# A graph network on one core: second edge bias in PSUM by ScalarE, edge layers in quarters, window additions first

## The reference, cut to what matters

```
h   = leaky(x @ W1[l] + b1[l]) @ W2[l] + b2[l]            # per node
e   = leaky(edge_attr @ We1[l] + be1[l]) @ We2[l] + be2[l] # per edge
msg = h[src] * e * dot_scale[l]
agg = segment_sum(msg, dst)
x   = layernorm(x + agg * res_w[l]) * ln_g[l] + ln_b[l]
```

## Time and profile before

| | |
|---|---|
| median of three runs | 6618.61 us |
| profiled execution, its own time | 6615.82 us |
| its span | 6614.0 us |
| busy: TensorE, VectorE, GpSimd, ScalarE | 85%, 78%, 68%, 17% |
| chain that ended last, by engine | TensorE 54%, VectorE 21%, issue 15%, ScalarE 3% |
| granted TensorE clock, mean | 0.88 of 2.4 GHz |

### The profile page before, as it was taken

How to read it: one execution, slowest core, us unless ns; L and a number is a source line. 1 busy time by engine, 2 the same in 40 slices (tenths; PEclk the granted TensorE clock), 3 DMA queues, 4 the chain that set the end, 5 groups by cost and what they waited for, 6 DMA issues and landing times.

```text
span 6614.0 us, 169076 instructions
## 1 busy us (share of the span) xinstructions
PE 5622.6 (85%) x63332; PEld 3676.7 (56%) x63333; DVE 5148.4 (78%) x7991; ACT 1133.9 (17%) x1726; POOL 4527.2 (68%) x4793
## 2 busy tenths in 40 slices
PE   6776899988888788888878888888898887888887
PEld 2223444456666555666655666655566665556665
DVE  8997544688887688888768888867888875888886
ACT  0000211111122211112211112221111222111111
POOL 5777777666677377777727777746777773777775
PEclk9997555799999799999979999988999997999998
DMA  3112399755566355656635655644565563666664
GB/s 135 26 26 47 78 240 242 185 131 138 138 148 152 96 132 136 142 141 154 159 80 133 145 143 143 162 112 116 129 147 142 148 161 78 139 147 156 151 171 110
DMA packets 733545, 886.20 MB, mean 134 GB/s; under 512 B 325488, under 2 KB 502976, under 8 KB 731568
## 3 DMA queue, kind: packets, MB, share of 16 engines
q1 hardware_dynamic: 568480, 703.64, 40.8%
q0 software_dynamic: 152144, 154.93, 12.4%
q10 hardware_dynamic: 12096, 16.53, 0.8%
HBM read 749.51 MB, written 125.06 MB: 132 GB/s over the span
## 4 chain that ended last, share of the span: by engine, by line
PE 54%; DVE 21%; issue 15%; DVEq 4%; ACT 3%; DMA 1%; POOL 0%; ACTq 0%; SPq 0%; POOLq 0%
PE bank L980 14%; PE bank L976 8%; PE bank L1029 7%; PE bank L1053 5%; PE bank L922 4%; PE bank L879 3%; DVE arena L1662 3%; PE bank L1016 3%; PE bank L860 2%; PE bank L845 2%; DVEq L1782 2%; DVE arena L1750 2%; ACT arena L1241 2%; DVE arena L1670 2%; DVE arena L1408 2%
## 5 line engine op out<-in xcount | busy, mean ns | idle before, releaser
L793 POOL DMA_INDIRECT arena<-h_rows,src x3855 | 3674.3, 953 | 1693.5 <-issue 1250.7
L980 PEld LDWEIGHTS bank<-w2s,arena 128*128 128x128 f32 x8960 | 1175.7, 210 | 772.3 <-DVE arena L1750 437.2
L980 PE MATMUL bank<-w2s,arena 128*128 128x128 f32 x8960 | 1307.0, 303 | 208.2 <-DVE arena L1750 191.4
L780 POOL DMA_INDIRECT slots<-arena,slot_index x792 | 787.2, 994 | 267.2 <-issue 241.3
L976 PE MATMUL bank<-nodes_state,edge_w 64*128 64x512 f32 x980 | 598.4, 693 | 307.3 <-DVE nodes_state L1718 142.6
L1053 PEld LDWEIGHTS bank<-arena 112*64 112x64 f32 x20160 | 640.4, 138 | 267.0 <-issue 245.1
L1053 PE MATMUL bank<-arena 112*64 112x64 f32 x20160 | 725.8, 225 | 60.1 <-issue 54.2
L976 PE MATMUL bank<-x_packed,edge_w 64*128 64x512 f32 x1260 | 740.1, 669 | 16.4 <-ACT std L1190 15.6
L1241 ACT ACTIVATE arena<-bank,tenth 128x512 f32<-128x512 f32 x490 | 335.5, 685 | 2296.6 <-PE bank L976 2296.6
L1662 DVE SCALAR_TENSOR_TENSOR arena<-bank,edge_w,arena 128x512 f32<-128x512 f32 x490 | 366.7, 748 | 424.1 <-ACT arena L1241 421.4
L1670 DVE TENSOR_TENSOR x_packed<-bank,slot_rel 128x2880 f32<-128x2880 f32 (+8 forms) x315 | 588.9, 1870 | 15.8 <-issue 15.8
(11 more groups left out here) (198 smaller groups left out, 5615.6 us busy)
## 6 DMA issues: line engine op xcount, KB each, us to landing
arena<-slot_pick SPq DMA_DIRECT2D x630, 448.0 KB
arena<-h_rows SPq DMA_DIRECT2D x630, 224.0 KB
x_packed<-slot_attr SPq DMA_DIRECT2D x630, 128.0 KB
nodes_state<-attr_t SPq DMA_DIRECT2D x485, 128.0 KB
arena<-h_rows,src POOLq DMA_INDIRECT x3855
slot_pick<-arena SPq DMA_DIRECT2D x126, 448.0 KB
x_packed<-slots SPq DMA_DIRECT2D x127, 136.0 KB, 4.9
slots<-arena SPq DMA_DIRECT2D x9, 1904.0 KB, 22.1
```

Of the source, the lines that this page charges most:

```text
L780: pool.indirect_dma_start(slots, bass.IndirectOffsetOnAxis(ap=slot_index[:, t:t + 1], axis=0), records[:, v, j, :], None).then_inc(record_ ...
L793: pool.indirect_dma_start(to[0:n, at:at + D], None, table, bass.IndirectOffsetOnAxis(ap=index[0:n, t:t + 1], axis=0)).then_inc(landed(t), 16)
L980: mm = pe.matmul(to[:, j * P:(j + 1) * P], acts[:, j * TILE:(j + 1) * TILE], w2s[:, :], start=True, stop=True)
```

## The change

ScalarE writes the second edge bias into `e_ps` and `slot_ps` (`bias`), as soon as the product that read the bank is done, and the matmuls of the second edge layer add onto it. VectorE's two bias passes go; ScalarE copies the slot group's edge values from `slot_ps` to `slot_e`. Where a step has both sorts at s+1, `edge_out_both` does them together in quarters of 64x64 on 64 columns that leave the zero quarters of `w2s` out: first half the gathered group from the upper 64 rows of the array while the slot group has the lower, second half the other way round, with a wait of TensorE on its own results between. The other steps keep `edge_out`. At each round's start eight matmuls of ones write both banks. VectorE reads the windows' addresses and adds the windows right behind the leaky passes, ahead of the slot one-hot, and no longer at the step's end. The declarations of semaphores, and the far pass, which no edge of this input needs and which keeps its bias on VectorE, are left out of the diff.

```
+    def pairs_before(s):
+        return sum(1 for j in range(-1, s) if a_at(j + 1) is not None and b_at(j + 1) is not None)
+
+    PAIRS = pairs_before(STEPS)
...
-            def edge_out(acts, to):
+            def edge_out(acts, to, onto_bias):
                 for j in range(TPH):
                     mm = pe.matmul(to[:, j * P:(j + 1) * P], acts[:, j * TILE:(j + 1) * TILE],
-                                   w2s[:, :], start=True, stop=True)
+                                   w2s[:, :], start=not onto_bias, stop=True, skip_group_check=onto_bias)
                 return mm
+
+            def edge_out_both(acts, slot_acts, pairs, onto_bias):
+                own_wait(pe, "pe")
+                for side in range(2):
+                    for j in range(TPH):
+                        for half in range(2):
+                            edges_of = slice(j * TILE + half * D, j * TILE + (half + 1) * D)
+                            outs = slice(half * D, (half + 1) * D)
+                            for k, to, of in ((side, e_ps, acts), (1 - side, slot_ps, slot_acts)):
+                                at, rows_of = (2 * j + k) * D, slice(k * D, (k + 1) * D)
+                                mm = pe.matmul(to[outs, at:at + D], of[rows_of, edges_of], w2s[rows_of, rows_of],
+                                               start=not onto_bias, stop=True, skip_group_check=onto_bias)
+                                if j == TPH - 1:
+                                    done = halves_out if side == 0 else e_ready if of is acts else slot_e_ready
+                                    mm.then_inc(done, 1)
+                    if side == 0:
+                        pe.wait_ge(halves_out, 4 * pairs)
+                        own_wait(pe, "pe")
...
+                pe.wait_ge(spill_attr_ready, 2)
                 own_wait(pe, "pe")
+                for to in (e_ps, slot_ps):
+                    for j in range(TPH):
+                        mm = pe.matmul(to[:, j * P:(j + 1) * P], ident[:, :], ones[:, :], start=(j == 0), stop=True,
+                                       skip_group_check=True)
+                mm.then_inc(banks_written, 1)
...
-                                           source_rows[0:ROWS, i % 2, k * D:(k + 1) * D], start=True, stop=True)
+                                           source_rows[0:ROWS, i % 2, k * D:(k + 1) * D], start=(k == 0), stop=True,
+                                           skip_group_check=True)
...
                     now, m = a_at(s), a_at(s + 1)
-                    if now == SPILL_AT:
-                        pe.wait_ge(spill_msg_ready, l + 1)
-                    elif now is not None:
-                        pe.wait_ge(msg_ready, l * GR + real(now) + 1)
+                    k = b_at(s + 1)
                     if m is not None:
                         pe.wait_ge(hid_acted[0], l * GA + m + 1)
-                        edge_out(hidden[:, 0, m % 2, :], e_ps).then_inc(e_ready, 1)
-                    k = b_at(s)
-                    if k is not None:
-                        pe.wait_ge(slot_msg_ready, l * NB + k + 1)
-                    k = b_at(s + 1)
+                        pe.wait_ge(e_begun, l * GA + m + 1)
                     if k is not None:
                         pe.wait_ge(hid_acted[1], l * NB + k + 1)
-                        edge_out(hidden[:, 1, k % 2, :], slot_ps).then_inc(slot_e_ready, 1)
+                        pe.wait_ge(slot_e_begun, l * NB + k + 1)
+                    if m is not None and k is not None:
+                        edge_out_both(hidden[:, 0, m % 2, :], hidden[:, 1, k % 2, :], l * PAIRS + pairs_before(s) + 1, True)
+                    elif m is not None:
+                        edge_out(hidden[:, 0, m % 2, :], e_ps, True).then_inc(e_ready, 2)
+                    elif k is not None:
+                        edge_out(hidden[:, 1, k % 2, :], slot_ps, True).then_inc(slot_e_ready, 2)
                     if now is not None and now != SPILL_AT:
+                        pe.wait_ge(msg_ready, l * GR + real(now) + 1)
                         pe.wait_ge(hid_acted[0], l * GA + a_before(s + 3))
                         window_sums(now)
                     if b_at(s) is not None:
-                        if k is None:
-                            own_wait(pe, "pe")
+                        pe.wait_ge(slot_msg_ready, l * NB + s + 1)
+                        own_wait(pe, "pe")
                         chunk_sums(s)
                     part("middle")
                     if k is not None:
-                        pe.wait_ge(slot_e_biased, l * NB + k + 1)
+                        pe.wait_ge(slot_e_kept, l * NB + k + 1)
...
+                act.wait_ge(banks_written, l + 1)
                 own_wait(act, "act")
 
+                def bias(to):
+                    return act.activation(to[:, :].rearrange("p (t f) -> p t f", f=D),
+                                          b2s[:, :].unsqueeze(1).to_broadcast((P, TPG, D)), ACT.Identity)
+
                 def step(s, part):
+                    now, m = a_at(s), a_at(s + 1)
+                    if now == SPILL_AT:
+                        act.wait_ge(spill_msg_ready, l + 1)
+                    elif now is not None:
+                        act.wait_ge(msg_ready, l * GR + real(now) + 1)
+                    if m is not None:
+                        bias(e_ps).then_inc(e_begun, 1)
+                    elif now is not None:
+                        own_wait(act, "act")
+                    i = b_at(s)
+                    if i is not None:
+                        act.wait_ge(slot_msg_ready, l * NB + i + 1)
+                    i = b_at(s + 1)
+                    if i is not None:
+                        bias(slot_ps).then_inc(slot_e_begun, 1)
+                    elif b_at(s) is not None:
+                        own_wait(act, "act")
                     for side, n, k in ((0, GA, a_at(s + 2)), (1, NB, b_at(s + 2))):
                         if k is not None:
                             act.wait_ge(hid_ready[side], l * n + k + 1)
                             hidden_tenth(side).then_inc(tenth_ready[side], 1)
+                    if i is not None:
+                        act.wait_ge(slot_e_ready, 2 * (l * NB + i + 1))
+                        act.activation(slot_e, slot_ps[:, :], ACT.Identity).then_inc(slot_e_kept, 1)
...
-                        dve.wait_ge(e_biased, l * GA + k + 1)
...
+                        dve.wait_ge(e_ready, 2 * (l * GA + k + 1))
...
-                        dve.wait_ge(slot_e_biased, l * NB + i + 1)
+                        dve.wait_ge(slot_e_kept, l * NB + i + 1)
...
@@ -1762,12 +1818,11 @@
                     for side, n, j in ((0, GA, a_at(s + 2)), (1, NB, b_at(s + 2))):
                         if j is not None:
                             acted(side, j, n)
-                    if i is not None:
-                        dve.wait_ge(slot_e_ready, l * NB + i + 1)
-                        edge_biased(slot_e, slot_ps[:, :]).then_inc(slot_e_biased, 1)
-                    if m is not None:
-                        dve.wait_ge(e_ready, l * GA + m + 1)
-                        edge_biased(e_ps[:, :], e_ps[:, :]).then_inc(e_biased, 1)
+                    if k is not None and k != SPILL_AT:
+                        group = GB0 + real(k)
+                        window_start[:] = [dve.value_load(start_i[0:1, 2 * group + side:2 * group + side + 1],
+                                                          min_val=0, max_val=NPAD) for side in range(2)]
+                        window_added(s, k)
                     part("middle")
...
-                    if k is not None and k != SPILL_AT:
-                        group = GB0 + real(k)
-                        window_start[:] = [dve.value_load(start_i[0:1, 2 * group + side:2 * group + side + 1],
-                                                          min_val=0, max_val=NPAD) for side in range(2)]
-                        window_added(s, k)
                     if ends_chunk(s):
                         chunk_added(s)
```

More of the change, by code:

```diff
@@ L335, in build @@
         e_ready, slot_e_ready, source_ready = sem("e_ready"), sem("slot_e_ready"), sem("source_ready")
-        e_biased, slot_e_biased = sem("e_biased"), sem("slot_e_biased")
+        e_begun, slot_e_begun, slot_e_kept, banks_written = sem("e_begun"), sem("slot_e_begun"), sem("slot_e_kept"), sem("banks_written")
         msg_ready, slot_msg_ready = sem("msg_ready"), sem("slot_msg_ready")
+        halves_out = sem("halves_out")
         win_ready, sum_ready, added = sem("win_ready"), sem("sum_ready"), sem("added")
@@ L989, in far_pass @@
                     pe.wait_ge(far_hid_acted, n + 1)
-                    edge_out(hidden[:, 0, 0, :], e_ps).then_inc(far_e_ready, 1)
+                    edge_out(hidden[:, 0, 0, :], e_ps, False).then_inc(far_e_ready, 1)
                     with pe.Fori(0, FW) as w:
```

## The result

The changed kernel takes 6989.89 us (median of 4 runs, 6973.32 to 6997.58), the kernel before in the same series 6619.2: ratio 1.0555, interval 1.0532 to 1.0578, slower by 371 us. The forecast was 6613, its range 6440 to 6760.

What follows compares the result with a forecast made beforehand. It took each step to be a ring of waits, with neither TensorE nor VectorE full. Steps +43, chunk ends -50, node tiles 0, rest +2 gave -5 on 6615.82; as a median 6613 us, range 6440 to 6760.

Steps and rivals of the forecast that it cites:

- 111: Step with a gathered group at s, s+1 and s+2; at width 360 forecast 8.52 us, from 8.13.
- 110: Step with a gathered group at s and s+1, none at s+2; at width 360 forecast 8.15 us, from 7.73.
- 101: Step with a gathered group at s and s+2, none at s+1; at width 360 forecast 7.93 us, from 6.90.
- 011: Step with a gathered group at s+1 and s+2, none at s; at width 360 forecast 7.11 us, from 8.32.
- +0.07 a step: Layer steps: net change taken for the new schedule of waits, times 620 steps = +43 us.
- Its 0.4 us saved buys nothing here: TensorE in the wide 111 step: the quarters' saving is worthless, as TensorE is done at 9.2, needed again at 10.6.
- Rival B: VectorE's queue at the window additions: they become the wait that ends last; +136 us, to 6750; chance 0.20.
- Rival C: TensorE's clock in the steps: granted clock falls to 0.90; +125 us, to 6740; chance 0.08.
- Chunk ends: Chunk additions: the slot one-hot hides the 1.31 us idle of their address reads; -50 us, bounds -60 and 0.
- Node tiles: The 11 or 12 tiles a layer inside the steps: gains and losses cancel; zero, 90 us either way.
- Rival D: TensorE's edge product: quarters run two at a time and lengthen it; +390 us, to about 7000; chance 0.02.
- rival A: VectorE's idle before leaky and additions is half that worked out; -155 us, to about 6455; chance 0.24.

Runs made afterwards that it cites:

- e5: Kernel before, with gathered and slot edge matmuls joined as eight whole 128x128 matmuls in turn, all waits in front: 6786.28 us, ratio 1.0254.
- W: The part that puts VectorE's window additions ahead of the slot one-hot; alone on the kernel before: 6550.21 us, ratio 0.9902.
- B: The part where ScalarE writes the edge bias and copies the slot result; alone on the kernel before: 6510.02 us, ratio 0.9847.
- e2: Kernel before with only the edge layers in joined quarters, bias staying on VectorE: 6760.31 us, ratio 1.0226.
- e6: e5 plus a stop of TensorE after four of the eight whole matmuls, until these have ended: 6928.97 us, ratio 1.0477.
- e3: Kernel before with only the window additions moved ahead of the slot one-hot: 6550.21 us, ratio 0.9902.
- e1: Changed kernel without quarters and moved additions, so only ScalarE's bias with its copy: 6510.02 us, ratio 0.9847.
- e17: Changed kernel with window and chunk additions put back to the step's end, keeping ScalarE's bias and quarters: 6795.73 us, ratio 1.0270.
- e8: e1 with VectorE reading the window and chunk addresses ahead of the leaky passes, additions staying last: 6479.75 us, ratio 0.9785.
- the second slow series: A repeat of four variants of the changed kernel's parts, with the kernel before at 11253.27 us; ratios 1.037, 1.032, 1.008 and 1.051, not used.

## Why the prediction was wrong, point by point

**The sizes of single operations were right.** ScalarE's write into PSUM: 0.603 us for the 0.63 taken. A half: 0.70 in most pairs, 0.80 on average (733.2 / 920), for 0.70. The stop: 133.2 / 460 = 0.29 us, a little over the 0.1 to 0.2. So the pair with its stop takes 1.89 us on average, where 1.55 was forecast; but eight whole matmuls in a row take 2.34 on average in e5, where 1.98 had been read, and the forecast saving of 0.4 us is there. The idle before the gathered leaky is 0.54 for 0.76 in the step shown, and 1.29 on average (634.5 / 490), for 0.87 before.

**The wide steps were right for two kinds of four.** Means of the first chunk over the middle three rounds, without the step that ends the chunk:

| kind | before | changed | forecast, from one step read before |
|---|---|---|---|
| 111 | 7.97 | 8.64 | 8.52, from 8.13 |
| 110 | 7.96 | 8.94 | 8.15, from 7.73 |
| 101 | 7.01 | 7.90 | 7.93, from 6.90 |
| 011 | 8.36 | 7.15 | 7.11, from 8.32 |

The 111 mean is near the forecast by averaging: one of the three 111 steps takes about 6.94 us in most rounds, and the one that was worked out takes 9.09, 0.57 more than forecast. In the 110 step the window sums stand behind the stop and both halves, and the additions wait 1.46 us (at 3618.82) where 0.82 had been worked out (free at 3.65, landed at 4.47). In the 111 step the wait also had another cause than the one given: address reads were to end it ("issue"), but they explain 17.5 of the 788 us; it was the window sums.

**The step that failed is the sum's "+0.07 a step" with its bounds -0.25 and +0.30.** Measured from the first slot product to the last, the steps of the middle three rounds went from 983.7 to 1064.7 us on average, or 0.65 a step; all five rounds grew by 361 of the 371 us. Even its own working gave more than it took: 7.89 against 7.74 is +0.15 for the wide steps, and the two narrow ones gave +0.05 and +0.51. Beyond that it failed in two places. "Its 0.4 us saved buys nothing here" put the quarters at nothing, from TensorE's free time in one wide 111 step. They cost 280, because they come with waits: the gathered group's matmuls now wait for the slot product and its bias, and both results land together at the end. The forecast followed these waits through the wide steps alone. And "at width 48 ... nothing is gained by width" came from two steps that are among the quick ones. They took 6.11 and 5.97 us for 5.93 and 5.67, but the mean 110 step of the last chunk (some hold parts of a node tile) went from 6.35 to 8.67. The last chunk's steps rose from 6.57 to 7.80 us, the first chunk's from 8.02 to 8.38. That the chain above is longest against the narrow steps would explain this; it was not tested by itself.

**Rival B was the mechanism of a large part, and it was priced too low.** It said that the additions become the wait that ends last, once window sums land after 4.8 us, at +136. W on top of B costs +198, and the wait is 1.62 us a group on average (787.8 / 485), over the 1.1 that was to show it. The row it turned on is in the timeline above: sums out at 3609.68, 4.71 us after the first product's start at 3604.97, and the additions at 4.97. The forecast had the sums landing at 4.52 and the additions free to start at 4.82. Only 0.3 us lay between, in one kind of step, before any node tile or slow clock; that should have moved chances to B.

**Rival C came true as well.** The steps' granted clock is 0.91 (0.95 in the earlier trace rows), under the 0.92 that was its sign. Half-clock time inside the steps rose from 450 to 887 us, all five rounds. In a fit over the 585 steps of each trace that end no chunk, by chunk, kind and tile part, each us at half clock goes with 0.4 us more (0.411 x 399 before, 0.388 x 826 after): 157 us of the 371. That is a fit, not an experiment. The quarters bring it: e2 has 758 us at half clock in the steps, e6, slower by 170 us, has 553.

**Chunk ends** went as forecast in kind: issue idle before the chunk additions 42.9 us before, 4.7 in e3, 3.4 in the changed kernel; but there 17.7 us of waiting for TensorE's chunk sums came instead. -50 was forecast; it is -38 at most. **Node tiles** were put at zero: steps 4 and 5 behind a tile's begin rose by 1.8 and 1.5 us, step 2, where the earlier trace rows had the 2.24 us, fell by 0.8. A part of it is VectorE's idle before the tile's own leaky and its product with the node matrix, which in the steps rose from 17 to 57 us and from 26 to 59.

**Rival D's number came out, its mechanism did not.** 6990 lies beside D's 7000, by coincidence: the halves take 0.80 us on average and not over 0.9, and the quarters' form saves time in both places where it was tried (-172 and -122).

**A slip in rival A.** By the forecast's own terms -155 takes the place of the +43, which gives 6416 and not 6455. Nothing here turns on it.

**The two rules.** ScalarE's passes by themselves are a gain (-107, e1); what costs is where they stand in the chain. The Trainium skill's "ScalarE: Activation LUTs" (Rules for kernel authors) gives adding to VectorE, and the price that the prediction drew from that was some +200 us; on this kernel, in float32, the run disagrees. And the clock: with the added waits of e6 it is 0.878, with the quarters 0.858. The Trainium skill has gaps between bursts as the cause of the slow clock ("TensorE: Matmul & The Clock Gate", HAM oscillation). The gaps of the two kernels are much alike. Their pairs, e6's and e2's:

```profile
L993 PE MATMUL bank<-w2s,arena 128*128 128x128 f32 x7360 | 1186.0, 310 | 329.3 <-DVE arena L1779 293.0 <-issue 8.4
```

```profile
L999 PE MATMUL bank<-w2s,arena 64*64 64x64 f32 x29440 | 724.9, 242 | 479.6 <-DVE arena L1778 252.1 <-PE bank L999 149.5 <-DVE arena L1785 45.3
```

e6's stop hardly stands as idle. It stands in the length of the pair, 0.30 us more on average than in e5, 138 us in all (0.30 x 460). With it the waiting before and in the pair is about 441 us in e6 (303 before it) and 480 in e2. So these waits do not tell why e2 has 205 us more at half clock. That leans to the quarters themselves, or to e2's pauses below; no run separates the two.

## What to carry to other kernels

Price a change of several parts as pairs too: B and W gained 107 and 67 us alone and lost 91 together, since one took away the work that hid the other's wait. When two matmul groups are joined to fill the array, price first what the earlier now waits for and what the later one's readers now wait for; here that was +315 against -172 for the form. And a schedule worked out for the wide steps says little for the narrow ones: here they grew more than three times as much (1.23 us a step against 0.36).

## What the runs showed of the hardware

- With four times as many matmul instructions in the pair, TensorE now and then pauses for no recorded reason. The page's queue of instructions went from 530 packets to:

```profile
q8 instruction: 710, 11.63, 0.7%
```

  Two examples of the changed kernel at width 360:

```profile
3613.83 0.69 PE L1083 MATMUL bank<-arena 112*64 112x64 f32 x16 [0.96 <-issue]
...
3618.48 3.48 PE L1059 MATMUL bank<-x_packed,arena 64*64 64x360 f32 x32
```

  In the first the second half of a group comes 0.96 us late; the second lasts 2.65 us elsewhere. By the packet records of that queue TensorE goes on 1.42 and 1.44 us after a 16 KB packet has landed. In all, 40 idle times of TensorE over 0.1 us that no other engine ended (33 us) end 1.3 to 1.5 us after such a packet, where the kernel before has 3 (0.6 us). e2 has 48 (35 us) and e6, with the same waits and whole matmuls, 3 (0.6 us): the pauses come with the quarters. So some 32 us of the 371. That the packets cause them was not tested by itself.
- ScalarE is no slower than VectorE at these sizes: 603 ns to write 128x512 f32 into PSUM (L1286), 597 to copy it out (L1313), 0.69 us for VectorE's add.
- The kernel before took 6613 us and 11127 us in two series. The transfers differed (the kernel of e17 moved a mean of 131 GB/s in one and 77 in the other), VectorE's instructions hardly (its slot product 685 and 687 ns). Why they differed is not known: e5 to e8 and the second slow series ran on the same chip.
